# Four groups of instructions in other places between the attention and the expert tiles

## The chip, the cores and the metric
The kernel runs on one core of one Trainium2 chip. The time is the device time of one execution in microseconds (us), the median over several. The core has five engines that run their own instruction streams and meet only at semaphores: TensorE (PE; its weight loads are a second row, PEld), VectorE (DVE), ScalarE (ACT), GpSimd (POOL) and SyncE (SP), which here only starts DMAs.

## The reference
One layer on an input of 8 batches x 256 tokens x 256: normalisation, attention with compressed keys and values (16 heads, a rotary part of 64), then a second normalisation and a mixture of experts, with two residual sums.

```
x = x + attention(layernorm(x))          # 16 heads, 8 batches of 256 tokens
h = layernorm(x)
logits  = h @ gate_w                     # 8 experts
scores  = softmax(logits)
top_w, top_i = top_k(scores, 2)
routed  = sum over the 2 chosen experts of top_w * (silu(h @ w_gate[e]) * (h @ w_up[e])) @ w_down[e]
shared  = (silu(h @ sw_gate) * (h @ sw_up)) @ sw_down      # hidden size 352
x = x + routed + shared
```

## The kernel before, in words
All products are made in three terms of rounded halves: `hi` is a tile rounded by a copy on ACT, `lo` the rest, subtracted on DVE or POOL (`minus_hi`, line 299), and a product is hi*hi + hi*lo + lo*hi (line 226, the helper `three`). So each tile that goes from one product to the next costs an ACT copy (line 1222) and a DVE subtraction.

The first stage is a loop over 64 pairs of heads (g = 0 to 63, eight to a batch). For a pair PE makes scores, ACT the exponentials `probs`, PE turns them (`turn`), ACT and DVE split them (`probs_hi`, `probs_lo`), PE multiplies them with the values (`attend`) into `ps_o`, and `norms` puts the inverse sums into the other half of `ps_o`. ACT copies these to `norm` (`norm_out`), DVE multiplies (`attended`, tile `on`), and `project` follows. `attend` of a pair waits for `norm_done`, since both use one bank. Beside this, the loop carries the router of the batch before: `turn_f` (transposes of the normalised rows `xhat` into `ps_m`), `turned_hi`/`turned_lo` (tile `xf`), `logits`, `gate_max`, `gate_exp` (exponentials `eprob` of 8 columns), `masks` (which two experts), `rank` (products with a triangular matrix that count, for each token, its place in its expert's list), `places` (the row numbers `slots`), and POOL's `scatter` of the rows to DRAM. Weights of the experts are split on the way by `split_hi` on ACT and `split_lo` on DVE (tiles `md_hi`, `md_lo` for the down matrices).

After the loop comes the passage to the tiles, written out by hand on each engine: the shared expert of batches 0 to 3 in chunks (b, m) (`gate_up(b, m)` and `down(b, m)` on PE, `silu` and `unit_hi` on ACT, `units` and `unit_lo` on DVE), and between them the rest of the router: `masks` and `places` of batch 6 (B - 2), all of batch 7 (B - 1), and the table of tiles (`table_counts`, `table_tiles`, `table_rows`, which end with `row_i`, the first row of each tile). SP waits for the table and for the scattered rows and then loads the rows of the 39 tiles (`load_rows`, tile `xg`). Then comes the tile loop (`rows_turn`, `rows_gate_up`, `units_turn`, `rows_down`), the shared expert of batches 4 to 7, and the gathers and stores.

The order on each engine is the order of the written calls, and every engine runs its instructions strictly in that order. An instruction that waits holds all behind it on its engine. ACT's functions Exp and Silu are in different tables: where the function changes, an `ACT_TABLE_LOAD` stands in the order; copies need none.

Of the kernel before, what the change touches and what calls it, by code (L numbers as in the profile page):

```python
# [13 lines left out]
B, S, D = 8, 256, 256  # L14
# [6 lines left out]
PAIRS = B * NP  # L21
# [26 lines left out]
def chunk_rows(m):  # L48
    return min(P, HS - m * P)
# [6 lines left out]
def tile(j):  # L56
    return slice(j * P, (j + 1) * P)
# [57 lines left out]
PARTS = 3 + 4 * KD  # L115
# [344 lines left out]
def splits_upto(L, n):  # L460
    return sum(len(splits) for _, splits in L.parts[0:n + 1])
# [288 lines left out]
def loop(nc, L, d):  # L750
    ev = L.events
    with ExitStack() as ctx:
# [87 lines left out]
        def gu_spot(n):  # L840
            return (L.ps_q, L.ps_s[1], L.ps_t[1])[n % 3]
# [10 lines left out]
        def routed(i, r):  # L852
            return r + 1 if i == B - 1 else r
# [4 lines left out]
        def batch(b):  # L858
            return 0 <= b < B

        def pair(g):
            return 0 <= g < PAIRS
# [77 lines left out]
        def _(pe):  # L940
# [94 lines left out]
            def rank(b):  # L1035
                pe.wait_ge(ev.masks_done, b + 1)

                for n, (terms, at) in enumerate((([(L.before, 0)], 0), ([(L.ones, 0), (L.before, 1)], 1), ([(L.ones, 0), (L.ones, 1)], 2))):
                    for m, (stat, j) in enumerate(terms):
                        last = nc.tensor.matmul(misc[:, 0, at * E:(at + 1) * E], stat[:, :], both[:, j, :], start=m == 0, stop=m == len(terms) - 1)  # L1040
                last.then_inc(ev.rank_full, 1)

            def gate_up(b, m):
                n = ES * b + m
                if m == 0:
                    pe.wait_ge(ev.in_loaded[b], 32)
                if n == 0:
                    pe.wait_ge(ev.qcos_done, PAIRS)
                    pe.wait_ge(ev.part_lo, splits_upto(L, 2))
                elif n == 1:  # L1050
                    pe.wait_ge(ev.exp_done, HEADS)
                elif n >= 3:
                    pe.wait_ge(ev.unit_done, n - 2)
                rows = chunk_rows(m)
                cols = slice(m * P, m * P + rows)
                for g in range(2):
                    last = three(gu_spot(n)[0:rows, g, :],
                                 [(L.sgu_hi[:, g * KD + k, cols], L.sgu_lo[:, g * KD + k, cols],
                                   shared_in[b][:, 0, k, :], shared_in[b][:, 1, k, :]) for k in range(KD)])
                last.then_inc(ev.gu_full, 1)  # L1060

            def down(b, m):
                n = ES * b + m
                pe.wait_ge(ev.ulo_done, n + 1)
                if n == 0:
                    pe.wait_ge(ev.exp_done, HEADS)
                if m == 0 and b >= 2:
                    pe.wait_ge(ev.acc_done, b - 1)
                rows = chunk_rows(m)
                for j in range(NT):  # L1070
                    last = three(ps_d[b % 2][:, j, :], [(u_hi[n % 3][0:rows, tile(j)], u_lo[n % 3][0:rows, tile(j)],
                                                       L.sd_hi[0:rows, m, :], L.sd_lo[0:rows, m, :])],
                                 start=m == 0 and j == 0, stop=m == ES - 1, skip=True)
                last.then_inc(ev.down_done, 1)
# [55 lines left out]
            for g in range(PAIRS):  # L1130
                i, r = divmod(g, NP)
# [48 lines left out]
            logits(B - 1)  # L1180
            down(1, 0)
            gate_up(2, 1)
            down(1, 1)
            gate_up(2, 2)
            rank(B - 1)
            down(1, 2)
            gate_up(3, 0)
            down(2, 0)
# [32 lines left out]
        def _(act):  # L1221
# [12 lines left out]
            def query_hi(g):  # L1234
                act.wait_ge(ev.qrot_done, g + 1)
                if g >= 2:
                    act.wait_ge(ev.s_full, 2 * g - 2)
                copy(q_hi[g % 2][:, :, :], qf[g % 2][:, :, :]).then_inc(ev.qhi_done, 1)

            def exps(h):  # L1240
                act.wait_ge(ev.max_done, h + 1)
                if h >= 3:
                    act.wait_ge(ev.t_full, h - 2)
                for j in range(NT):
                    last = nc.scalar.activation(probs[h % 3][:, j, :], L.ps_s[h % 2][:, j, :], ACT.Exp,  # L1245
                                                bias=nmax[:, h % NH, j:j + 1], accum_out=rsum[:, h % NH, j:j + 1])
                last.then_inc(ev.exp_done, 1)

            def probs_hi(h):
                act.wait_ge(ev.t_full, h + 1)  # L1250
                if h >= 3:
                    act.wait_ge(ev.pv_done, h - 2)
                copy(pT_hi[h % 3][:, :, :], turned[h % 2][:, :, :]).then_inc(ev.phi_done, 1)

            def norm_out(g):
                act.wait_ge(ev.norm_full, g + 1)
                if g >= 1:
                    act.wait_ge(ev.on_done, g)
                copy(norm[:, :], L.ps_o[:, 1, :]).then_inc(ev.norm_done, 1)

            def attended_hi(g):
                act.wait_ge(ev.on_done, g + 1)
                if g >= 2:
                    act.wait_ge(ev.out_done, g - 1)
                copy(o_hi[g % 2][:, :], on[g % 2][:, :]).then_inc(ev.ohi_done, 1)
# [12 lines left out]
            def turned_hi(b):  # L1278
                act.wait_ge(ev.xf_turned, b + 1)
                if b >= 1:  # L1280
                    act.wait_ge(ev.xf_stored, 16 * b)
                    act.wait_ge(ev.logits_full, b)
                copy(xf_hi, misc[:, :, :]).then_inc(ev.xfhi_done, 1)
# [8 lines left out]
            def silu(b, m):  # L1292
                n = ES * b + m
                rows = chunk_rows(m)
                act.wait_ge(ev.gu_full, n + 1)
                if n >= 2:
                    act.wait_ge(ev.unit_done, n - 1)
                nc.scalar.activation(gate[n % 2][0:rows, :], gu_spot(n)[0:rows, 0, :], ACT.Silu).then_inc(ev.silu_done, 1)
# [48 lines left out]
            for g in range(PAIRS):  # L1347
                i, r = divmod(g, NP)
                exps(2 * g + 1)
                if pair(g + 2):  # L1350
                    query_hi(g + 2)
                if pair(g - 1):
                    probs_hi(2 * (g - 1) + 1)
                if pair(g - 2):
                    attended_hi(g - 2)
                if pair(g + 1):
                    exps(2 * (g + 1))
                if pair(g - 1):
                    norm_out(g - 1)
                if r == 4 and batch(i - 1):  # L1360
                    normal_f(i - 1)
                if (r == 0 and i >= 1 or g == 1) and batch(i + 1):
                    prep_normal(i + 1)
                if g in part_round:
                    split_hi(part_round[g])
                if r == 2 and batch(i + 1):
                    prep_x(i + 1)
                if r == 5 and batch(i + 1):
                    prep_k(i + 1)
                if routed(i, r) == 6 and batch(i - 1):  # L1370
                    turned_hi(i - 1)
                if routed(i, r) == 7 and batch(i - 1):
                    gate_exp(i - 1)
                if pair(g + 4):
                    swap(g + 4)
                probs_hi(2 * g)
            probs_hi(HEADS - 1)
            attended_hi(PAIRS - 2)
            silu(0, 0)
            norm_out(PAIRS - 1)  # L1380
            silu(0, 1)
            unit_hi(0, 0)
            attended_hi(PAIRS - 1)
# [40 lines left out]
        def _(dve):  # L1424
# [3 lines left out]
            split_lo = part_lo(nc, L, dve)  # L1428
# [91 lines left out]
            def tokens(b):  # L1520
                if b == 1:
                    dve.wait_ge(ev.cleared, 16)
                if b >= 2:
                    dve.wait_ge(ev.scattered[b % 2], 64 * (b // 2))
                vec.tensor_scalar(xhat_of[b][:, :, D], L.token[:, :], float(b * TOP * S), None, ALU.add).then_inc(ev.tags_done, 1)
# [59 lines left out]
            def unit_lo(b, m):  # L1585
                n = ES * b + m
                rows = chunk_rows(m)
                dve.wait_ge(ev.uhi_done, n + 1)
                if n >= 3:
                    dve.wait_ge(ev.down_done, n - 2)  # L1590
                minus_hi(u_lo[n % 3][0:rows, :], unit[n % 2][0:rows, :], u_hi[n % 3][0:rows, :]).then_inc(ev.ulo_done, 1)
# [66 lines left out]
            for g in range(PAIRS):  # L1658
                i, r = divmod(g, NP)
# [57 lines left out]
            units(1, 1)  # L1717
            places(B - 2)
            tokens(B - 1)
            unit_lo(1, 0)  # L1720
            units(1, 2)
            split_lo(PARTS + 3)
            turned_lo(B - 1)
            accumulate(0)
            unit_lo(1, 1)
# [175 lines left out]
```

## Time and profile before

| what | us |
|---|---|
| median of 3 runs | 628.88 (627.64 to 630.49) |
| the profiled execution | 629.82 |
| its span, first to last instruction | 628.1 |
| PE busy | 605.3 (96%) |
| ACT busy | 475.0 (76%) |
| DVE busy | 467.8 (74%) |
| POOL busy | 410.2 (65%) |
| mean granted clock of PE | 0.984 |

Times in the rows are us from the start of the span. A row of the timeline has the start, the time, the engine, the line of the kernel, the operation, output and inputs by their names (buffer numbers left out), the sizes and the count; in brackets stands the idle time of the engine just before it and what ended it. The granted clock is a share of 2.4 GHz: 1.00 is full speed, 0.50 is 1.2 GHz.

### The profile page before, as it was taken

To read this page: it belongs to the slowest core of one execution; us is meant where nothing else is said; L and a number is where in the kernel's file an instruction comes from. 1 tells how busy PE (TensorE), PEld (TensorE's weight loads), DVE (VectorE), ACT (ScalarE), POOL (GpSimd) and SP (SyncE) were. 2 spreads that over 40 slices of the span, in tenths; PEclk is the share of its full clock that TensorE was granted. 3 is DMA by queue.
4 is the path that set the end of the run, shared out by engine and by line. 5 is a ranking of instruction groups with operands and counts; after the bars stand their busy time and mean duration, and the time that the engine had idled before them with its cause. 6 is when DMAs were issued, how large, how long until landed. Compare 5 with 4: busy or idle time off the path is not lost. (4 is left out here: it accounts for less than half of the span.)

```text
span 628.1 us, 15730 instructions
## 1 busy us (share of the span) xinstructions
PE 605.3 (96%) x4916; PEld 591.3 (94%) x4916; DVE 467.8 (74%) x1406; ACT 475.0 (76%) x1331; POOL 410.2 (65%) x455
## 2 busy tenths in 40 slices
PE   8998999999999999999999999999979989999995
PEld 8888999999999999999999999999978979999994
DVE  6667786877886878788688887778666676666486
ACT  4779999898988989889898898979864335556531
POOL 1467897786897889789789978978613204444400
PEclk9998999999999999999999999999999889999998
DMA  9792000000001001000100100020603155444292
GB/s 259 238 345 41 2 1 3 2 1 35 11 10 43 11 18 43 10 19 3 43 18 10 43 9 19 9 78 11 184 2 118 51 173 166 124 132 120 86 320 83
DMA packets 34024, 45.41 MB, mean 72 GB/s; under 512 B 4056, under 2 KB 29112, under 8 KB 33944
## 3 DMA queue, kind: packets, MB, share of 16 engines
q1 hardware_dynamic: 29160, 34.56, 17.6%
q0 software_dynamic: 3408, 9.34, 4.6%
q8 instruction: 42, 0.69, 0.5%
q10 hardware_dynamic: 1376, 0.50, 0.3%
q14 instruction: 38, 0.31, 0.2%
HBM read 27.57 MB, written 16.82 MB: 71 GB/s over the span
## 5 line engine op out<-in xcount | busy, mean ns | idle before, releaser
L1245 ACT ACTIVATE probs<-ps_s,nmax 128x256 f32<-128x256 f32 x256 | 119.1, 477 | 10.8 <-DVE nmax L1439 10.7
L1785 POOL TENSOR_TENSOR qswap<-qswap,qsin 128x512 f32<-128x512 f32 x64 | 83.3, 1301 | 43.6 <-ACT qswap L1222 43.6
L226 PE MATMUL ps_q<-xa,wq_hi 128*128 128x256 f32 x512 | 101.0, 295 | 3.7 <-DVE qf L1434 3.7
L1439 DVE TENSOR_REDUCE nmax<-ps_s 128x2 f32<-128x512 f32 x128 | 86.8, 678 | 9.3 <-PE ps_s L226 8.6
L1222 ACT ACTIVATE pT_hi<-ps_t 128x512 fp32r<-128x512 f32 x128 | 76.7, 599 | 17.0 <-PE ps_t L978 15.6
L1788 POOL TENSOR_TENSOR qf<-qf,qswap 128x512 f32<-128x512 f32 x64 | 82.7, 1292 | 10.5 <-DVE qf L1434 6.5
L1792 POOL TENSOR_TENSOR q_lo<-qf,q_hi 128x512 fp32r<-128x512 f32 x64 | 82.9, 1296 | 5.8 <-ACT q_hi L1222 5.8
L226 PEld LDWEIGHTS ps_q<-xa,wq_hi 128*128 128x128 f32 x512 | 79.9, 192 | 5.5 <-DVE qf L1434 3.3
L299 DVE TENSOR_TENSOR pT_lo<-ps_t,pT_hi 128x512 fp32r<-128x512 f32 x128 | 81.9, 681 | 1.5 <-ACT pT_hi L1222 1.5
L226 PE MATMUL ps_o<-pT_hi,kv_hi 128*128 128x256 f32 x256 | 76.7, 300 | 2.5 <-ACT norm L1222 2.5
L226 PE MATMUL ps_s<-kT_hi,q_hi 128*128 128x256 f32 x256 | 77.6, 303 | 0.9 <-ACT probs L1245 0.9
L978 PE MATMUL ps_t<-ident,probs 128*128 128x128 f32 x512 | 76.8, 273 | 1.3 <-DVE pT_lo L299 1.3
L1222 ACT ACTIVATE qswap<-ps_q 32x512 f32<-32x512 f32 x128 | 75.6, 590 | 3.3 <-PE ps_q L226 1.0
L1813 POOL DMA_INDIRECT routed_out<-yb,to x39 | 37.4, 959 | 57.7 <-DVE to L1574 55.1
L226 PE MATMUL ps_q<-xa,wq_lo 128*128 128x256 f32 x256 | 73.0, 285 | 0.0
L226 PE MATMUL ps_s<-kT_hi,q_lo 128*128 128x256 f32 x256 | 71.9, 281 | 0.0
L226 PE MATMUL ps_s<-kT_lo,q_hi 128*128 128x256 f32 x256 | 71.8, 280 | 0.0
L226 PE MATMUL ps_o<-pT_hi,kv_lo 128*128 128x256 f32 x256 | 71.5, 279 | 0.0
L226 PE MATMUL ps_o<-pT_lo,kv_hi 128*128 128x256 f32 x256 | 71.4, 279 | 0.0
L978 PEld LDWEIGHTS ps_t<-ident,probs 128*128 128x128 f32 x512 | 59.4, 141 | 1.7 <-issue 1.7
L1796 POOL TENSOR_TENSOR o_lo<-on,o_hi 128x256 fp32r<-128x256 f32 x64 | 47.3, 739 | 17.9 <-ACT o_hi L1222 17.5
L1434 DVE TENSOR_TENSOR qf<-ps_q,qcos 128x512 f32<-128x512 f32 x64 | 43.7, 683 | 15.8 <-ACT qswap L1222 15.6
(337 smaller groups left out, 1914.5 us busy)
## 6 DMA issues: line engine op xcount, KB each, us to landing
xg<-routed_in SPq DMA_DIRECT2D x39, 129.0 KB, 2.2
normal_turned<-xf SPq DMA_DIRECT2D x8, 512.0 KB, 2.8
wq_raw<-Wq_dram SPq DMA_DIRECT2D x16, 192.0 KB, 4.5
x<-x_dram SPq DMA_DIRECT2D x8, 256.0 KB, 5.7
xa<-normal_turned SPq DMA_DIRECT2D x4, 512.0 KB, 5.5
mgu_hi<-routed_out SPq DMA_DIRECT2D x4, 512.0 KB, 5.2
mgu_lo<-routed_out SPq DMA_DIRECT2D x4, 512.0 KB, 7.9
out_dram<-x SPq DMA_DIRECT2D x8, 256.0 KB, 2.9
```

Of the source, the lines that this page charges most:

```text
L226: last = nc.tensor.matmul(out, stat, mov, start=start and n == 0, stop=stop and n == len(terms) - 1, skip_group_check=skip)
L299: return vec.tensor_tensor(lo, src, hi.bitcast(F32), ALU.subtract)
L978: last = nc.tensor.transpose(turned[h % 2][:, c, tile(j)], probs[h % 3][:, j, tile(c)], L.ident[:, :])
L1222: copy = lambda out, src: nc.scalar.activation(out, src, ACT.Copy)
L1245: last = nc.scalar.activation(probs[h % 3][:, j, :], L.ps_s[h % 2][:, j, :], ACT.Exp, bias=nmax[:, h % NH, j:j + 1], accum_out=rsum[:, h % ...
L1434: vec.tensor_tensor(qf[g % 2][:, :, :], L.ps_q[:, :, :], L.qcos[:, :].unsqueeze(1).to_broadcast([P, 2, S]), ALU.mult).then_inc(ev.qcos_don ...
L1439: vec.tensor_reduce(nmax[:, h % NH, :], L.ps_s[h % 2][:, :, :], AX.X, ALU.max, negate=True).then_inc(ev.max_done, 1)
L1785: gp.tensor_tensor(qs, qs, L.qsin[:, :].unsqueeze(1).to_broadcast([P, 2, S]), ALU.mult).then_inc(ev.qrot_part, 1)
L1788: gp.tensor_tensor(to, to, qs, ALU.add).then_inc(ev.qrot_done, 1)
L1792: gp.tensor_tensor(q_lo[g % 2][:, :, :], qf[g % 2][:, :, :], q_hi[g % 2][:, :, :].bitcast(F32), ALU.subtract).then_inc(ev.qlo_done, 1)
L1796: gp.tensor_tensor(o_lo[g % 2][:, :], on[g % 2][:, :], o_hi[g % 2][:, :].bitcast(F32), ALU.subtract).then_inc(ev.olo_done, 1)
L1813: gp.indirect_dma_start(ys[:, :], bass.IndirectOffsetOnAxis(to[:, j:j + 1], 0), yb[j % 3][:, :], None).then_inc(ev.y_stored[j % 3], 16)
```

## The change
Four calls change places; no call is added or taken away, and no wait of a call is changed. On PE `rank(B - 1)` goes ahead of `down(1, 1)` and `gate_up(2, 2)`. On ACT `gate_exp(B - 2)` leaves the loop (it ran at pair g = 62) and stands behind it, and `norm_out(PAIRS - 1)` goes ahead of `silu(0, 0)`. On DVE `split_lo(PARTS + 3)` goes ahead of `unit_lo(1, 0)` and `units(1, 2)`.

```diff
--- before.py
+++ after.py
@@ -1180,9 +1180,9 @@
             logits(B - 1)
             down(1, 0)
             gate_up(2, 1)
+            rank(B - 1)
             down(1, 1)
             gate_up(2, 2)
-            rank(B - 1)
             down(1, 2)
             gate_up(3, 0)
             down(2, 0)
@@ -1369,15 +1369,16 @@
                     prep_k(i + 1)
                 if routed(i, r) == 6 and batch(i - 1):
                     turned_hi(i - 1)
-                if routed(i, r) == 7 and batch(i - 1):
+                if routed(i, r) == 7 and batch(i - 1) and i < B - 1:
                     gate_exp(i - 1)
                 if pair(g + 4):
                     swap(g + 4)
                 probs_hi(2 * g)
             probs_hi(HEADS - 1)
             attended_hi(PAIRS - 2)
+            gate_exp(B - 2)
+            norm_out(PAIRS - 1)
             silu(0, 0)
-            norm_out(PAIRS - 1)
             silu(0, 1)
             unit_hi(0, 0)
             attended_hi(PAIRS - 1)
@@ -1717,9 +1718,9 @@
             units(1, 1)
             places(B - 2)
             tokens(B - 1)
+            split_lo(PARTS + 3)
             unit_lo(1, 0)
             units(1, 2)
-            split_lo(PARTS + 3)
             turned_lo(B - 1)
             accumulate(0)
             unit_lo(1, 1)
```

ACT, end of the attention loop and start of the passage. `eprob` are the router's exponentials of batch 6, `norm` the copy of the last pair's inverse sums, `gate` the first of the shared expert. The order on ACT before:

```order
L469 ACTIVATE md_hi<-md_raw 88x2x256 x2
L1288 ACTIVATE eprob,esum<-ps_m,lmax 128x8 x2
L1222 ACTIVATE pT_hi<-ps_t 128x512
...
L1222 ACTIVATE o_hi<-on 128x256
L1298 ACT_TABLE_LOAD
L1298 ACTIVATE gate<-ps_q 128x256
L1222 ACTIVATE norm<-ps_o 128x256
L1298 ACTIVATE gate<-ps_s 128x256
```

The same place on ACT after:

```order
L469 ACTIVATE md_hi<-md_raw 88x2x256 x2
L1222 ACTIVATE pT_hi<-ps_t 128x512
L1245 ACTIVATE probs,rsum<-ps_s,nmax 128x256 x2
...
L1222 ACTIVATE o_hi<-on 128x256
L1288 ACTIVATE eprob,esum<-ps_m,lmax 128x8 x2
L1222 ACTIVATE norm<-ps_o 128x256
L1298 ACT_TABLE_LOAD
L1298 ACTIVATE gate<-ps_q 128x256
```

The exponentials went from behind the weight split to behind `o_hi`, and `norm` from between the first two gates to ahead of the table load.

DVE, the passage, at batch 6's places and the split `xf` of batch 7. The order on DVE before:

```order
L1518 COPY xhat_f<-row_f 128x2
L1525 TENSOR_SCALAR xhat_g<-token 128x2
L299 TENSOR_TENSOR u_lo0<-unit1,u_hi0 128x256
L1583 TENSOR_TENSOR unit1<-ps_t1,gate1 96x256
L477 TENSOR_TENSOR md_lo<-md_raw,md_hi 88x2x256 x2
L299 TENSOR_TENSOR xf<-ps_m,xf 128x512
L1596 TENSOR_TENSOR x2<-ps_s0,x2 128x512
```

The same place on DVE after:

```order
L1519 COPY xhat_f<-row_f 128x2
L1526 TENSOR_SCALAR xhat_g<-token 128x2
L477 TENSOR_TENSOR md_lo<-md_raw,md_hi 88x2x256 x2
L299 TENSOR_TENSOR u_lo0<-unit1,u_hi0 128x256
L1584 TENSOR_TENSOR unit1<-ps_t1,gate1 96x256
L299 TENSOR_TENSOR xf<-ps_m,xf 128x512
L1597 TENSOR_TENSOR x2<-ps_s0,x2 128x512
```

The subtraction `md_lo` went from right ahead of `xf` to ahead of `u_lo` and the unit of chunk (1, 2).

PE, the passage, between the up products of chunk (2, 1) (`ps_s`) and of (2, 2) (`ps_t` from `wo_hi`; the shared expert's inputs of batch 2 lie in `wo_hi`). The order on PE before:

```order
L226 MATMUL ps_s<-wo_hi,sgu_lo 128x256
L226 MATMUL ps_t<-sd_hi,u_hi 128x256
...
L226 MATMUL ps_t<-sd_hi,u_lo 128x256
L226 MATMUL ps_t<-wo_hi,sgu_hi 96x256 x2
L226 MATMUL ps_t<-wo_hi,sgu_lo 96x256
...
L226 MATMUL ps_t<-wo_hi,sgu_lo 96x256
L1040 MATMUL ps_m<-both,before 128x8
L1040 MATMUL ps_m<-both,ones 128x8
L1040 MATMUL ps_m<-both,before 128x8
L1040 MATMUL ps_m<-both,ones 128x8 x2
```

The same place on PE after:

```order
L226 MATMUL ps_s<-wo_hi,sgu_lo 128x256
L1040 MATMUL ps_m<-both,before 128x8
L1040 MATMUL ps_m<-both,ones 128x8
L1040 MATMUL ps_m<-both,before 128x8
L1040 MATMUL ps_m<-both,ones 128x8 x2
L226 MATMUL ps_t<-sd_hi,u_hi 128x256
...
L226 MATMUL ps_t<-sd_hi,u_lo 128x256
L226 MATMUL ps_t<-wo_hi,sgu_hi 96x256 x2
L226 MATMUL ps_t<-wo_hi,sgu_lo 96x256
...
L226 MATMUL ps_t<-wo_hi,sgu_lo 96x256
L226 MATMUL ps_t<-sd_hi,u_hi 128x256
```

The counting products (line 1040) went ahead of `down(1, 1)` (`ps_t` from `u_hi`, `u_lo`) and of `gate_up(2, 2)`.

## Rows read from the trace of the kernel before

**Rows 1.** Stretch 510:594: us, busy us (x instructions) of each engine, clock, DMA share, GB/s
```profile
510.00:594.00 84.00, 83.81 (x622) 81.17 (x621) 52.99 (x190) 48.19 (x154) 35.95 (x38) 1.00 0.46 139
```

**Rows 2.** PE's waits, 455 to 530: total us, times, longest us
```profile
PE ps_o L226 <- ACT norm L1222: 2.1, 1, 2.1
...
PE ps_t L226 <- DVE u_lo L299: 2.0, 1, 2.0
```

**Rows 3.** PE by time: start us, us, engine, line, operation, tiles, count, [idle before <-releaser]
```profile
481.45 0.66 PE L1025 MATMUL ps_m<-ident,xhat_g 128*128 128x128 f32 x4
...
484.57 0.27 PE L226 MATMUL ps_m<-gw_hi,xf 128*128 128x8 f32 x1 [1.04 <-DVE xf L299]
...
493.34 0.17 PE L1040 MATMUL ps_m<-both,before 128*128 128x8 f32 x1
...
506.23 0.69 PE L1081 MATMUL ps_m<-ident,xg 128*128 128x128 f32 x2 [1.75 <-DMA xg<-routed_in]
```

**Rows 4.** DVE by time, 481 to 503
```profile
481.73 0.42 DVE L299 TENSOR_TENSOR u_lo<-unit,u_hi 128x256 fp32r<-128x256 f32 x1 [1.20 <-ACT u_hi L1222]
...
482.60 1.31 DVE L477 TENSOR_TENSOR md_lo<-md_raw,md_hi 88x512 fp32r<-88x512 f32 x2
...
483.84 0.68 DVE L299 TENSOR_TENSOR xf<-ps_m,xf 128x512 fp32r<-128x512 f32 x1
...
486.48 0.17 DVE L1484 TENSOR_REDUCE lmax<-ps_m 128x2 f32<-128x16 f32 x1 [1.03 <-PE ps_m L226]
...
489.28 0.17 DVE L1504 TENSOR_TENSOR choice<-both,choice 128x16 f32<-128x16 f32 x1
...
494.00 0.17 DVE L1510 TENSOR_TENSOR where<-ps_m,base 128x16 f32<-128x16 f32 x1 [3.88 <-PE ps_m L1040]
...
502.95 0.17 DVE L1558 CAST row_i<-row_of 1x39 int32<-1x39 f32 x1
```

**Rows 5.** SyncE's wait for the scattered rows (line 926)
```profile
L926 SPq EVENT_SEMAPHORE  x1: 28/28/28, 502.7 to 502.7; - x1
```

**Rows 6.** Three stretches, as rows 1; the clock follows POOL's busy time
```profile
485.00:495.00 10.00, 10.00 (x61) 10.00 (x61) 4.08 (x32) 3.64 (x10) 1.16 (x1) 0.66 0.22 81
...
495.00:500.00 5.00, 5.00 (x44) 5.00 (x44) 4.78 (x16) 1.49 (x4) 3.28 (x4) 1.00 0.16 57
...
505.00:510.00 5.00, 3.77 (x19) 3.74 (x20) 3.12 (x15) 1.07 (x3) 0.00 (x0) 0.66 0.43 109
```

**Rows 7.** ACT by time, 459 to 482
```profile
459.52 0.27 ACT L1288 ACTIVATE eprob<-ps_m,lmax 128x8 f32<-128x8 f32 x1 [1.44 <-DVE lmax L1484]
...
460.03 0.59 ACT L1222 ACTIVATE pT_hi<-ps_t 128x512 fp32r<-128x512 f32 x1
...
460.51 0.48 ACT L1245 ACTIVATE probs<-ps_s,nmax 128x256 f32<-128x256 f32 x1
...
467.38 0.41 ACT L1222 ACTIVATE o_hi<-on 128x256 fp32r<-128x256 f32 x1
...
467.80 1.28 ACT L1298 ACT_TABLE_LOAD   x1
...
469.10 0.38 ACT L1298 ACTIVATE gate<-ps_q 128x256 f32<-128x256 f32 x1
...
469.38 0.38 ACT L1222 ACTIVATE norm<-ps_o 128x256 f32<-128x256 f32 x1
...
482.14 0.60 ACT L1222 ACTIVATE xf<-ps_m 128x512 fp32r<-128x512 f32 x1 [0.17 <-PE ps_m L1025]
```

**Rows 8.** DVE by time, 459 to 479
```profile
459.41 0.68 DVE L1439 TENSOR_REDUCE nmax<-ps_s 128x2 f32<-128x512 f32 x1
...
471.58 0.42 DVE L1466 TENSOR_TENSOR on<-ps_o,norm 128x256 f32<-128x256 f32 x1 [0.74 <-PE ps_o L226]
...
474.13 0.42 DVE L1583 TENSOR_TENSOR unit<-ps_t,gate 96x256 f32<-96x256 f32 x1 [0.57 <-ACT gate L1298]
...
479.03 0.16 DVE L317 TENSOR_SCALAR var_f<-mean_f 128x2 f32<-128x2 f32 x1
```

## The prediction

> **What bounds the kernel now.** I read first the busy time by stretch. In the stage of the 39 expert tiles TensorE (PE) is busy for 83.81 of 84 us [rows 1], so that stage can't absorb or return anything: it starts when its first tile is there and ends a fixed time later. The passage before it is another matter. The waits of PE between 455 and 530 us [rows 2] start with 2.1 us for the copy `norm` and 2.0 us for VectorE's (DVE's) `u_lo`; a third is 1.75 us for the DMA of the first tile, `xg` [rows 3]. In the last two PE waits for a chain that runs on DVE; so for the start of the tiles the question is not how much PE idles, but what that chain waits for. I followed it backwards. The transposes of the first tile start at 506.23 behind that DMA wait [rows 3], 3.1 us after DVE finished `row_i`, the row numbers that its load reads (502.95 + 0.17) [rows 4]; the scattered rows were there by then, since SyncE's wait for them ended at 502.7 [rows 5]. `row_i` stands at the end of table work that starts with `where` at 494.00, and from there DVE has nothing to wait for. `where`, the first step of the places of the last batch (7), had DVE idle for 3.88 us, released by PE's counting products [rows 4], which start at 493.34 [rows 3]. But the masks that these count were ready with `choice` at 489.45 (489.28 + 0.17) [rows 4]. About 4 us of the chain are thus only PE's order of work. A second view is PE's granted clock [rows 6]: 1.00 (2.4 GHz) at 495:500 with 44 products, but 0.66 over 485:495 with 61, where 88 would fit, and 0.66 at 505:510. 0.66 over 10 us is 6.8 us at 1.2 GHz, and the 27 missing products are worth 3.1 us. So PE runs most of the stretch ahead of the counting at half clock; the clock fell there after a 1.04 us wait and in the middle of the narrow, eight-column router products [rows 3].
>
> **The change part by part.** Nothing is added or removed; four groups change places.
>
> 1. Router exponentials of batch 6 on ScalarE (ACT). They stood at 459.52 with 1.44 us idle before them, and the next `probs` pair came at 460.51 [rows 7]. That pair also needs the row maxima, which DVE ends at 459.41 + 0.68 = 460.09 [rows 8]; DVE's own order doesn't change there. So `probs` starts at 460.13: 0.38 gained, not 1.44, and what follows (DVE's sums, PE's transposes) moves by that amount.
>
> 2. The copy `norm` before the table load. `o_hi` started at 467.38 [rows 7] and now starts at 467.00. Behind it come the four small exponential instructions, which take 0.51 us as a group (459.52 to the `pT_hi` at 460.03) [rows 7]; then `norm`. One ACT start follows the last by 0.28 (469.10 to 469.38) to 0.42 (467.38 to 467.80) [rows 7]; with 0.33 this gives 467.00 + 0.33 + 0.51 = 467.84 against 469.38 [rows 7]: PE's attention products go on 1.54 us earlier, and 0.6 of the 2.1 us of [rows 2] stays. The exponentials find the exponential table still in place, since the load that they stood ahead of is now behind them. Price: the table load and the first `gate` behind it come at 469.56 instead of 469.10 [rows 7]. It meets DVE's `unit` and `u_lo` work ahead of the last `on`; that chain moves later by 0.46, then catches up, since `unit_hi` follows the second gate, which lost its place only by 0.2. I work out that `on`, at 471.58 [rows 8], comes at 471.23, 0.35 earlier. From there DVE had one more wait, 0.57 us before the `unit` of 474.13 [rows 8], for a gate of PE products that now come 1.54 us earlier. Both together: the masks of batch 6, the residual and `var_f` (479.03 [rows 8]) move by 0.9 to 1.0, not 1.54. `var_f` feeds GpSimd's power, ACT's normalisation and PE's transposes at 481.45, which followed the products ahead of them with hardly a pause (no wait is noted in their row [rows 3]). So here the gain is cut to 1.0: transposes at 480.45, with PE waiting 0.5 more than before.
>
> The row of the load says 1.28 us, and the first gate starts 1.30 after it [rows 7]. The Trainium skill (ScalarE: Activation LUTs, "What ACT_TABLE_LOAD costs") gives about 2.66 us for a switch of sets, drain included. By that the gate after the load would be 1.4 us later and DVE's chain the same; the trace does not agree, and the sum goes by the row.
>
> 3. The weight split (`md_lo`) on DVE. It took 1.31 us from 482.60 and stood right ahead of `xf_lo`, which began at 483.84 [rows 4]; the logits waited for that till 484.57 with PE idle 1.04 us [rows 3]. Now the split runs before `unit_lo`, where DVE had 1.2 us idle waiting for ACT ([rows 4], before 481.73; the split falls at 479.5 to 480.8 in the new times, and the rounded half that it needs comes from ACT before its normalisation, as now). Then `xf_lo` follows ACT's `xf`, which starts 0.69 after the transposes (482.14 [rows 7] against 481.45): 481.14, and 0.60 and 0.68 later `xf_lo` is done, 482.46 with the hand-overs. PE's gate and up products between transposes and logits end at about 482.5. So the wait of 1.04 goes entirely and the logits start at 482.5, 2.07 earlier than 484.57.
>
> 4. The counting products (rank) before `down(1,1)` and `gate_up(2,2)` on PE. From the logits to `lmax` the trace has 1.91 us (484.57 to 486.48, partly at half clock); at 44 products in 5 us, 0.114 each [rows 6], the twelve products and the reader's start take 1.5, so `lmax` comes at 484.1, and the masks, 2.97 us after it as before (486.48 to 489.45 [rows 4]), at 487.05. PE fills this with `down(1,0)` and `gate_up(2,1)`, 18 products, 2.1 us, to 486.1 and then waits 0.9 us: a new wait, behind which all PE work is queued. The counting starts at 487.1, `where` at 487.78 (0.66 later, as 493.34 to 494.00). That is 6.2 us earlier than 494.00. Behind it the DVE chain needs `down(1,2)` for the second accumulation at 490.6: PE gives it at 490.5 (24 products after 487.6), just in time. The slots, the scatter, `row_i` (496.9) and the load all move by the same 6.2, and the first tile's transposes come at 500.0. PE reaches them at about 498.3 and still waits 1.7, so DVE's chain and not PE sets this start. Without the move of rank alone, the counting would start at 488.2: of the 6.2 us, 1.1 belong to this edit at full clock, and much more (over 3) at half clock.
>
> Bounds of what the trace doesn't show. If PE has 2.4 GHz everywhere in the passage: 6.2; and if the second fall, at 505:510, stays away too, up to 1.5 more (0.66 over 5 us is 3.4 us at half clock [rows 6], at the 0.45 per us of case D). If the clock falls as before: 4.0 to 4.9 (next part). I take 6.2, because the wait that preceded the fall is taken away.
>
> Sum: the profiled execution took 629.82 us with a span of 628.1; minus 6.2 is 623.6. The median of the unprofiled runs, 628.88, is 0.9 lower; from it the sum is 622.7. I take the middle, 623.2.
>
> **The rivals.**
>
> A. The clock still falls. For it: the eight-column products, 12 of the logits and 5 of the count, now stand closer together, with new waits of 0.5 to 0.8 us ahead of the transposes and 0.9 us ahead of the count. Against: the 1.04 us wait directly ahead of the logits is gone, and the 2.1 us wait for `norm` [rows 2] was followed by no fall. In this case the 24 products to `down(1,2)` take about 0.2 instead of 0.114 each (28 products fit in the 3.2 us at full clock of 485:495, which leaves 33 for the 6.8 slow ones [rows 6]) and the accumulation comes about 2 us late; the gain is 4.0 to 4.9, in the middle 4.4: 625.4 from the profiled time, 624.5 from the median. The Trainium skill (TensorE: Matmul & The Clock Gate, Part 1) says that the activity monitor is free-running and does not start over with the kernel. By that rule some executions of the same program would fall and others not, which would also spread the runs; the three of before lie 2.9 us apart, and no trace here shows the cause.
>
> B. The logits do not come earlier, because the chain to `xf_lo` has a step that I mis-sized; only the move of rank pays. PE would count at 490.1 instead of 493.3, and the accumulation behind it is late by 0.7: 2.6 gained, 627.2 or 626.3. Against it: every wait in the chain has its row.
>
> C. No change: another stage takes the gain back, for instance the gathers at the end, or the copy is late for another reason, or the edits don't do what they say. Against: PE in the tiles is busy throughout [rows 1]. The time is then 628.9, give or take 1.5.
>
> D. Slower. The place is the start of the tiles: PE still waits twice there, 0.6 and 1.7 us, and the first tiles hold transposes and waits. If the clock falls there and does not come back at 509, as it did, but stays low over several tiles, each us at half clock costs about 0.45 us of work (3.1 for 6.8 [rows 6]). From 14 us of it on the whole gain is lost; at 25 us the cost is 11.3, and the time 5.1 above the median before, 634.0. Against: in [rows 6] the second fall was over within 5 us, and the tiles are dense.
>
> **How the numbers follow.** Forecast 50% (its own range 621.5 to 624.8), A 27%, B 10%, C 8%, D 5%. A measurement of this kernel tells a change from about 0.5%, 3.1 us: faster means under 625.7. That holds for the forecast and nearly all of A, and for little else: 0.79. Within 0.5% are B, C and an edge of A: 0.16. Slower: 0.05. The range goes from 621.0 (the second fall partly gone) to 626.4, where B ends from the median.
>
> **What would show it.** In the profile after: `norm` at about 467.8, ahead of the table load, and PE's wait for it under 1 us; `var_f` near 478.1 and the transposes at 480.4; logits at 482.5 with no wait before them; a new PE wait of about 0.9 us before the counting products, starting at 487.1; DVE's 3.88 us before `where` gone; the first tile's transposes at 500.0. The granted clock in 483 to 492 decides between forecast and A. The forecast is wrong if the first tile starts later than 503, or if it starts at 500 and the span doesn't follow.

## The result and the profile after

The changed kernel takes 624.40 us (median of 6, 622.67 to 625.89) against 629.43 us of before (6 runs, 627.64 to 630.49): ratio 0.9925, 95% interval 0.9905 to 0.9944. Forecast were 623.2 and a chance of 0.79 for faster. Two later sets of runs on two different chips gave ratios of 0.9909 (0.9873 to 0.9945) and 0.9912 (0.9879 to 0.9946). The profiled execution took 624.46 us with a span of 622.7.

The waits of PE between 450 and 525 us, to be read against [rows 2] and the brackets of [rows 3]:

```profile
PE ps_m L1081 <- DMA xg<-routed_in: 1.8, 1, 1.8
PE ps_o L226 <- ACT norm L1222: 0.9, 1, 0.9
PE ps_t L978 <- DVE pT_lo L299: 0.9, 1, 0.9
PE ps_m L1040 <- DVE choice L1505: 0.8, 1, 0.8
PE ps_m L1025 <- ACT xhat_g L1275: 0.6, 1, 0.6
PE ps_t L226 <- DVE u_lo L299: 0.4, 1, 0.4
```

PE's wait for `norm` is 0.9 instead of 2.1 us, the one for `u_lo` 0.4 instead of 2.0, and the wait ahead of the logits is not in the list. Two waits are new or longer: 0.8 for the counting products (line 1040) and 0.6 for the transposes (line 1025). The one ahead of the first tile is still there, 1.8 us.

PE by time, the rows that answer to [rows 3]:

```profile
479.50 0.66 PE L1025 MATMUL ps_m<-ident,xhat_g 128*128 128x128 f32 x4 [0.60 <-ACT xhat_g L1275]
...
481.57 0.27 PE L226 MATMUL ps_m<-gw_hi,xf 128*128 128x8 f32 x1
...
486.14 0.27 PE L1040 MATMUL ps_m<-both,before 128*128 128x8 f32 x1 [0.84 <-DVE choice L1505]
...
499.38 0.44 PE L1081 MATMUL ps_m<-ident,xg 128*128 128x128 f32 x2 [1.82 <-DMA xg<-routed_in]
```

DVE by time, for [rows 4] and [rows 8] (line numbers are one higher):

```profile
458.57 0.68 DVE L1440 TENSOR_REDUCE nmax<-ps_s 128x2 f32<-128x512 f32 x1
...
470.30 0.42 DVE L1467 TENSOR_TENSOR on<-ps_o,norm 128x256 f32<-128x256 f32 x1
...
472.19 0.41 DVE L1584 TENSOR_TENSOR unit<-ps_t,gate 96x256 f32<-96x256 f32 x1
...
477.08 0.16 DVE L317 TENSOR_SCALAR var_f<-mean_f 128x2 f32<-128x2 f32 x1
...
478.49 1.28 DVE L477 TENSOR_TENSOR md_lo<-md_raw,md_hi 88x512 fp32r<-88x512 f32 x2
...
480.82 0.69 DVE L299 TENSOR_TENSOR xf<-ps_m,xf 128x512 fp32r<-128x512 f32 x1
...
483.11 0.17 DVE L1485 TENSOR_REDUCE lmax<-ps_m 128x2 f32<-128x16 f32 x1 [0.66 <-PE ps_m L226]
...
485.91 0.17 DVE L1505 TENSOR_TENSOR choice<-both,choice 128x16 f32<-128x16 f32 x1
...
486.90 0.17 DVE L1511 TENSOR_TENSOR where<-ps_m,base 128x16 f32<-128x16 f32 x1 [0.15 <-PE ps_m L1040]
...
496.03 0.17 DVE L1559 CAST row_i<-row_of 1x39 int32<-1x39 f32 x1
```

ACT at the table load, for [rows 7]:

```profile
466.14 0.41 ACT L1222 ACTIVATE o_hi<-on 128x256 fp32r<-128x256 f32 x1
466.45 0.26 ACT L1288 ACTIVATE eprob<-ps_m,lmax 128x8 f32<-128x8 f32 x1
...
466.93 0.39 ACT L1222 ACTIVATE norm<-ps_o 128x256 f32<-128x256 f32 x1
467.34 1.28 ACT L1298 ACT_TABLE_LOAD   x1
468.63 0.38 ACT L1298 ACTIVATE gate<-ps_q 128x256 f32<-128x256 f32 x1
```

All of this run is 0.84 us ahead before the change begins: the last row maxima in the loop come at 458.57 instead of 459.41 [rows 8], after instructions that are the same in both kernels. In the twelve further profiles below that point lies between 457.1 and 461.0 us; two profiles of the changed kernel differ there by 3.35 us. So I count the passage from there. From these maxima to the first tile's transposes it took 506.23 - 459.41 = 46.82 us before and 499.38 - 458.57 = 40.81 after: 6.0 us less. PE's busy time splits this into two halves. The first line is before, the second after; both have 289 products:

```profile
459.41:506.23 46.82, 38.39 (x289) 36.93 (x289) 32.08 (x130) 21.67 (x55) 11.17 (x13) 0.92 0.17 60
```
```profile
458.57:499.38 40.81, 35.32 (x289) 33.88 (x288) 31.95 (x130) 21.11 (x54) 11.55 (x13) 1.00 0.20 69
```

PE idles 5.5 instead of 8.4 us, 2.9 less, and is busy 3.1 us less with the same products, at a clock of 1.00 instead of 0.92.

The rest of the way did not stay the same. Stretches of the profile after, as [rows 6] (the clock is the third number from the end):

```profile
466.00:476.00 10.00, 9.07 (x77) 8.86 (x76) 6.44 (x30) 5.80 (x18) 1.46 (x2) 1.00 0.15 47
485.00:495.00 10.00, 9.16 (x78) 8.95 (x77) 9.21 (x43) 3.77 (x11) 4.12 (x4) 1.00 0.19 69
500.00:507.50 7.50, 7.46 (x32) 6.77 (x31) 4.02 (x13) 2.23 (x7) 0.00 (x0) 0.54 0.65 189
510.00:590.00 80.00, 79.96 (x600) 77.87 (x599) 48.98 (x177) 45.81 (x147) 37.08 (x39) 1.00 0.42 126
```

The clock stays at 1.00 where it was 0.66 before (485:495), but from 500 to 507.5 it is 0.54, that is 6.9 us at 1.2 GHz, where before had 3.4. From the first tile to the end this execution needs 123.3 us and the one before 121.9. The balance of the two profiles: 0.8 by the start, 6.0 in the passage, 1.5 given back from the tiles on: 5.4 us of span. The longer fall is not all of the 1.5, as the further profiles of both kernels show below.

### The profile page after: what moved, and what is told of

Same layout as the page of the kernel before. It is cut to its first block and busy times, and to the rows that moved or that the text cites. A ratio compares the mean times of both kernels' runs of the same rounds, so it can differ in the third digit from the quotient of the medians.

```text
span 622.7 us, 15730 instructions
## 1 busy us (share of the span) xinstructions
PE 601.9 (97%) x4916; PEld 587.2 (94%) x4916; DVE 469.0 (75%) x1406; ACT 474.8 (76%) x1331; POOL 410.4 (66%) x455
## 3 DMA queue, kind: packets, MB, share of 16 engines
HBM read 27.57 MB, written 16.82 MB: 71 GB/s over the span
## 5 line engine op out<-in xcount | busy, mean ns | idle before, releaser
L1435 DVE TENSOR_TENSOR qf<-ps_q,qcos 128x512 f32<-128x512 f32 x64 | 43.7, 683 | 15.6 <-ACT qswap L1222 15.4
```

What stands on the lines that cost most here:

```text
L1435: vec.tensor_tensor(qf[g % 2][:, :, :], L.ps_q[:, :, :], L.qcos[:, :].unsqueeze(1).to_broadcast([P, 2, S]), ALU.mult).then_inc(ev.qcos_don ...
```

## The experiments

Each ratio is to runs of the kernel before on the same chip. For every execution the mean granted clock is known, and with it its time at 1.2 GHz: (1 - clock) x span x 2; the clock is given to 0.001, so this comes in steps of about 1.25 us. "Passage" is the time from the last row maxima to the first tile, from the profile.

| kernel | ratio (95%) | median us | us at 1.2 GHz, median | passage us |
|---|---|---|---|---|
| before, 67 runs in three sets | 1 | 629.5 | 17.6 | 46.82, 46.76, 46.79 |
| changed, 18 runs in three sets | 0.9925, 0.9909, 0.9912 | 624.2 | 8.7 | 40.81, 40.80, 40.75 |
| ACT edits alone | 0.9954 (0.9928 to 0.9979) | 625.7 | 13.7 | 42.75 |
| split alone | 0.9956 (0.9925 to 0.9988) | 625.3 | 15.0 | 44.10 |
| count alone | 0.9983 (0.9954 to 1.0012) | 626.9 | 15.6 | 43.35 |
| ACT and split | 0.9927 (0.9899 to 0.9955) | 623.6 | 12.4 | 41.62 |
| count one place later | 0.9927 (0.9901 to 0.9952) | 624.5 | 14.9 | 40.65 |
| changed, filled at the tiles | 0.9907 (0.9874 to 0.9940) | 622.9 | 7.4 | 40.76 |
| before, filled at the logits | 0.9976 (0.9953 to 1.0000) | 627.5 | 16.2 | 45.14 |
| count later, filled twice | 0.9895 (0.9863 to 0.9928) | 621.8 | 6.8 | 40.53 |

**The ACT edits alone.** The edit:

```diff
-                if routed(i, r) == 7 and batch(i - 1):
+                if routed(i, r) == 7 and batch(i - 1) and i < B - 1:
                     gate_exp(i - 1)
...
+            gate_exp(B - 2)
+            norm_out(PAIRS - 1)
             silu(0, 0)
-            norm_out(PAIRS - 1)
```

> Only the two edits on ACT: the router's exponentials of batch 6 behind the loop, the copy norm ahead of the table load. Theory (the chain sets the start of the tiles; each edit pays by what it moves there): PE's wait for norm falls from 2.1 to about 0.9 us, the transposes of batch 7 come 1.0 earlier, the logits 1.0 earlier and still after a 1 us wait behind the weight split, the clock falls as before, and DVE's 3.9 us before `where` stay. Time 1.0 us under before, ratio 0.998. Rival (PE's waits count): 1.5 us or more, ratio 0.9975 or less.

The steps came as forecast: the transposes come 20.94 us after the row maxima, before 22.04, so 1.1 earlier, and the logits still wait. But the clock did not fall. PE ahead of the logits and the clock after them in this profile:

```profile
482.93 0.27 PE L226 MATMUL ps_m<-gw_hi,xf 128*128 128x8 f32 x1 [1.05 <-DVE xf L299]
```
```profile
466.00:476.00 10.00, 9.07 (x78) 8.86 (x77) 6.17 (x29) 5.83 (x17) 1.47 (x2) 1.00 0.12 32
483.00:495.00 12.00, 12.00 (x103) 12.00 (x104) 8.98 (x46) 5.14 (x14) 4.35 (x6) 1.00 0.24 89
```

The wait of 1.05 us is there, the eight-column products are there, and the clock stays at 1.00. So the two together do not make it fall in every execution, and my reason for the forecast ("the wait that preceded the fall is taken away") is not the whole of it. The passage is 4.1 us shorter, 1.1 by order and 3 by the clock of this execution. The time is 3.7 us under before, where 1.0 was expected, and the interval just leaves out the expected 0.998. The number is in the rival's range, but the order of work moved the chain by the theory's 1.1 us; the rest goes with the clock (13.7 us at 1.2 GHz in the median against 17.6).

**The split alone.**

```diff
+            split_lo(PARTS + 3)
             unit_lo(1, 0)
             units(1, 2)
-            split_lo(PARTS + 3)
```

> Only the weight split ahead of unit_lo(1, 0) on DVE. Theory: the wait ahead of the logits goes, they start 1.0 us earlier. If the clock's fall hung on that wait, PE stays at 2.4 GHz up to the counting products, which then come 4 us earlier: ratio 0.9935. Rival (the clock falls in any case, by the narrow products): 1.0 us, ratio 0.998.

From the transposes to the logits it took 2.07 us instead of 3.12: 1.05 us by order, as forecast. At the logits the clock stayed up. But this execution had a fall that the first profile of before did not have, behind the 2.13 us wait for `norm` (466:476):

```profile
466.00:476.00 10.00, 8.39 (x58) 8.42 (x59) 4.84 (x26) 3.88 (x10) 1.03 (x2) 0.83 0.01 2
480.00:495.00 15.00, 14.85 (x126) 14.45 (x125) 11.77 (x51) 8.69 (x22) 7.57 (x8) 1.00 0.25 89
```

This fall made DVE's chain up to the transposes 1.5 us late. The ratio lies between the two expectations, and its interval holds both, so the time decides nothing between them.

**The counting products alone.**

```diff
+            rank(B - 1)
             down(1, 1)
             gate_up(2, 2)
-            rank(B - 1)
```

> Only the counting products ahead of down(1, 1) and gate_up(2, 2) on PE. Theory: the clock falls as before; the products come at about 490.1 against 493.3, without a wait; the second accumulation is 0.7 late; 2.6 us gained, ratio 0.996. Rival (PE's order does not matter): no gain, ratio 1.000.

The passage shrank by 3.5 us in the profile, but part of that is a shorter fall (clock 0.79 over 484:492, that is 3.4 us at 1.2 GHz instead of 6.8). The time, 0.9983 where 0.996 was expected, does not tell it from no change. The logits started at 484.87, and `where` followed 5.76 us later:

```profile
490.63 0.17 DVE L1510 TENSOR_TENSOR where<-ps_m,base 128x16 f32<-128x16 f32 x1 [0.58 <-PE ps_m L1040]
```

At full clock that way takes 5.33 us with the count in its new place (the changed kernel) and 6.34 in its old one (the next run). So here a fall of 3.4 us cost the chain 0.4 us. A fall of the same length behind the logits of the kernel before cost it 1.5 (7.87 us, 486.48 to 494.35, in the first of the two further profiles below). The earlier count is thus worth about 2 us where the clock falls behind the logits, and 1.1 at `where` (0.8 at the first tile) where it does not. The prediction had 1.1 at full clock and "over 3" at half clock, for a fall twice as long.

**The changed kernel without the move of the count.** The edit is the last diff taken back.

> The changed kernel with the counting products put back behind gate_up(2, 2). Theory: the clock stays up in the passage as in the changed kernel, the new PE wait of 0.84 us goes, the counting starts 1.1 us later than in the changed kernel, and so does the first tile: ratio to before 0.9943 (the changed kernel 0.9925). Rival (the rank edit is the larger part of the gain): 3 us later than the changed kernel, 0.997.

The counting starts 28.69 us after the maxima instead of 27.57, 1.1 later as forecast, and the first tile 0.8 later (41.62 against 40.81): of the 1.1, 0.1 went between the count and `where`, and 0.2 in DVE's wait for the second accumulation, both in the changed kernel. In the time nothing of it is seen: 0.9927 against 0.9909 to 0.9925. The clock is 1.00 in this passage up to 497.0, shortly ahead of PE's wait for the first tile, and falls there:

```profile
496.50:504.00 7.50, 5.96 (x27) 5.64 (x28) 5.13 (x18) 1.49 (x4) 0.00 (x0) 0.54 0.35 92
```

**The changed kernel once more**, on the chip of the next three.

> The changed kernel once more, on the chip of the next three. Every execution has its own count of us at 1.2 GHz, (1 - mean clock) x span x 2, and before loses 0.46 us for each. Theory: the changed kernel gains 3 us by its order of work at equal clock, and 1 to 2 us more since the clock falls less often in the passage: ratio 0.9925, 3 us under before at equal us of low clock. Rival (all of it is the clock): no difference at equal us of low clock.

Ratio 0.9909; the passage 40.80. Its clock is 1.00 from 482 to 512, at the start of the tiles too, and from the first tile to the end it needs 122.3 us, 1.0 less than the first profile. Over all 18 runs of the changed kernel the median is 8.7 us at 1.2 GHz, over the 67 of before 17.6. The 0.41 us per us that a line through the 67 runs gives makes about 3.6 us of this difference. The comparison at equal clock is thin, since the two hardly overlap: between 10 and 14.5 us at 1.2 GHz lie 14 runs of before with a median of 625.8 and 4 of the changed kernel with 624.4. 11 of the 18 have 10 us or less, and 1 of the 67.

So the expected 3 us at equal clock were not found in the times: it is 1.4 here, and the 18 runs lie on average 1.6 us under the line of the kernel before (for most of them the line has to be drawn on below its own points). Against that the kernel "ACT and split" lies 3.0 under the line, and "count one place later" 2.9. The rival, that all is clock, is out by the passage, but how the time divides into order and clock is not settled.

The stretch from the first tile to the end has a part in this. It took 121.9, 122.3 and 122.3 us in the three profiles of before, with 3.4, 6.8 and 6.8 us at 1.2 GHz around the first tile, and 123.3, 122.3 and 122.4 in the three of the changed kernel, with 6.9, none and none. With the same fall the changed kernel needs 1 us more there, and without a fall as much as before with one. The 20 us from the first tile, before and in this run:

```profile
506.23:526.23 20.00, 19.85 (x133) 18.96 (x134) 12.97 (x47) 10.06 (x32) 4.79 (x5) 0.92 0.70 213
```
```profile
501.77:521.77 20.00, 19.20 (x131) 17.34 (x132) 12.70 (x45) 9.82 (x32) 4.79 (x5) 1.00 0.67 206
```

At full clock PE idles 0.8 us there (1.3 in the third profile) instead of 0.15. So part of what the passage gained is given back behind it. Which order of work costs it there was not tested.

**The count one place later.**

```diff
-            rank(B - 1)
             down(1, 1)
+            rank(B - 1)
             gate_up(2, 2)
```

> The changed kernel with the counting products between down(1, 1) and gate_up(2, 2). They are ready when their masks are, which is after down(1, 1) would end, so they start at the same time as in the changed kernel. Theory: PE's new wait of 0.84 us ahead of them shrinks to 0.1, the first tile comes at the same time after DVE's last row maxima (40.8 us), or 0.2 earlier, since down(1, 2) comes 0.7 earlier for the second accumulation. Time as the changed kernel or up to 0.5 us less. Rival: the wait counts, 0.8 us less.

The products start at the same 27.57 us, now without PE's wait of 0.84, and the first tile comes 0.15 earlier. The wait has moved: PE's wait for `u_lo` is 1.0 us instead of 0.4. The time is 624.5 against 623.7 on the same chip, where the same or up to 0.5 less was expected; the intervals overlap. Its median of time at 1.2 GHz is 14.9 us against 8.1 of the changed kernel beside it. The new wait of the change costs the start of the tiles 0.15 us at most, since DVE's chain is what ends last.

**Idle products at the start of the tiles.**

```diff
+            def filler(count):
+                pe.wait_ge(ev.x2_done, B)
+                for n in range(count):
+                    nc.tensor.matmul(L.ps_y[:, 0, :], L.sgu_hi[:, 0, 0:P], L.sgu_lo[:, 0, 0:S], start=True, stop=True)
...
             down(3, 0)
+            filler(15)
             rows_turn(0)
```

> The changed kernel with 15 idle products (128x128 weights, 256 columns, into a bank that nobody reads) in the 1.8 us in which PE waits for the first tile. They add work only. Theory (a fall of the clock at the tile start follows the waits just before it, and costs 0.45 us for each us at 1.2 GHz): the clock stays at 1.00 through 500:510, the us of low clock fall by about 7 and the time by 1.5 to 3 us against the changed kernel. Rival (the fall has nothing to do with the wait): the same clock, and time as the changed kernel or up to 0.5 more.

PE in this profile, with the idle products in the place of the wait:

```profile
496.26 1.95 PE L1088 MATMUL ps_y<-sgu_lo,sgu_hi 128*128 128x256 f32 x15
498.18 0.44 PE L1081 MATMUL ps_m<-ident,xg 128*128 128x128 f32 x2
```

The clock stayed at 1.00, but so it did in the unfilled kernel's second and third profiles, and the medians differ by 0.8 us, where 1.5 to 3 were expected, with intervals that overlap. The time at 1.2 GHz hardly moved either (7.4 against 8.1 us, expected about 7 less). This neither shows nor refutes the theory that the wait brings the fall; its price is not borne out.

**Idle products ahead of the logits, in the kernel before.** `filler(8)` ahead of `logits(B - 1)`.

> The kernel before with 8 idle products in PE's 1.04 us wait ahead of the logits of batch 7. Theory (the fall at 485 follows this wait): the clock stays up through 483:495 in most executions, the high cluster of times (630 to 632) thins out, median 1.5 to 3 us under before. Rival (the fall comes in any case, by the narrow products or by chance of position): distribution as before, ratio 1.000.

In the profile there is no fall after the logits (483:495), but one behind the wait for `norm` (466:476):

```profile
466.00:476.00 10.00, 7.87 (x54) 7.66 (x53) 3.86 (x12) 4.58 (x10) 1.46 (x2) 0.83 0.01 2
483.00:495.00 12.00, 11.91 (x102) 11.71 (x101) 8.94 (x45) 6.84 (x16) 4.35 (x6) 1.00 0.24 89
```

Of the 12 runs none is above 630 us, where 8 of the 21 unfilled ones on this chip are (25 of all 67). The median is 2.0 us lower and the ratio's interval just touches 1. That speaks for the theory, which had 1.5 to 3 us, without settling it: the one profile has no fall behind the logits, but neither has that of the ACT edits alone, where the wait was left as it was.

**Two more profiles of the kernel before.**

> The kernel before, unchanged, one more profile. Theory (the place where the clock falls is not fixed by the program): the passage from DVE's last row maxima in the loop to the first tile takes 43.7 us where the clock stays at 1.00 and 46.8 where it falls as in the first profile; the fall may be absent from 485:492 or stand at another place. Rival (the program fixes it): 0.5 at 486 to 492 again, and 46.8.

> The kernel before once more, one more profile, with the same expectations as the look before it.

The first of them, around the two waits:

```profile
469.00:476.00 7.00, 5.71 (x35) 5.74 (x36) 2.38 (x5) 2.87 (x8) 0.73 (x1) 0.76 0.01 2
486.00:492.00 6.00, 5.52 (x34) 5.52 (x35) 4.10 (x25) 3.26 (x10) 1.89 (x2) 0.72 0.43 156
```

and the second:

```profile
469.00:476.00 7.00, 6.72 (x44) 6.75 (x45) 3.18 (x11) 1.88 (x6) 0.73 (x1) 0.76 0.01 2
486.00:492.00 6.00, 6.00 (x40) 6.00 (x40) 3.09 (x24) 3.26 (x9) 1.16 (x1) 0.72 0.37 134
```

There are two falls now, 3.4 us at 1.2 GHz each (0.24 x 7 x 2 and 0.28 x 6 x 2): one behind the wait for `norm`, where the first profile had none, and one behind the logits as in the first, half as long. In the first of the two profiles the logits started here:

```profile
486.48 0.27 PE L226 MATMUL ps_m<-gw_hi,xf 128*128 128x8 f32 x1 [1.05 <-DVE xf L299]
```

The second fall follows 1.5 us later (in the very first profile 1.0 after the logits' start). So the program does not fix whether the clock falls at a wait nor for how long, but the places are the same few. The passage is 46.76 and 46.79, as long as the first: three profiles of before, 6.8 us at 1.2 GHz in each, and three of the changed kernel with none. The theory's 43.7 us at full clock was not seen in any profile of before.

All fourteen profiles together show something that the forecast did not have. In the six without the ACT edits (where PE waits 2.1 us for `norm`) the clock fell between that wait and the count every time. In the eight with them (where it waits 0.9) it never did, also not in the one where the wait of 1.05 us ahead of the logits was left. So the smaller share of low clock in the passage goes with the ACT edits in these profiles. No run shows how they bring it about.

**Both ideas together**: the count one place later, 7 idle products ahead of `down(3, 0)` and 15 ahead of the first tile, and beside it the changed kernel again.

> The changed kernel with the counting products between down(1, 1) and gate_up(2, 2), 7 idle products ahead of down(3, 0) and 15 ahead of the first tile's transposes. Theory: first tile at 40.65 us after DVE's last row maxima, clock 1.00 to 510, fewer us of low clock than the changed kernel (8 to 11): median 622.5 to 623.2, 0.5 to 1.5 under the changed kernel on the same chip. Rival (the idle products only delay): as the changed kernel or more.

> The changed kernel, beside the last one on its chip. Theory: first tile again 40.8 us after DVE's last row maxima, ratio 0.991 to 0.9925. Rival: a ratio above 0.994, if the two chips so far were kind to it.

The first tile came at 40.53 and 40.75 us, and the medians are 621.8 and 623.2 on one chip, 1.4 apart as expected (0.5 to 1.5). It is the lowest median of all, but its interval (0.9863 to 0.9928) overlaps with the other's. The changed kernel's 0.9912 is as its theory had it.

## Why the prediction was right

By its own steps, each as us from the last row maxima (459.41 in the forecast's times):

| step | forecast | measured |
|---|---|---|
| `norm` starts | 8.43 | 8.36 |
| `var_f` (478.05) | 18.6 | 18.51 |
| transposes of batch 7 | 21.04 | 20.93 |
| logits | 23.1 | 23.00 |
| masks ready | 27.6 | 27.51 |
| counting products | 27.7 | 27.57 |
| `where` | 28.37 | 28.33 |
| `row_i` ends | 37.5 | 37.63 |
| first tile | 40.6 | 40.81 |

- The exponentials' new place gave `probs` 0.39 (0.38 forecast), `norm` comes 1.6 earlier with it, and of this 1.1 was left at the transposes, since DVE's chain of batch 6 holds them, as forecast. The new PE wait there is 0.60 (0.5 more was said). PE's wait for `norm` is 0.93, not the forecast's 0.6: the sum took the copy's whole gain off the wait, though PE comes to it 0.4 earlier too.
- The split's move took the whole wait ahead of the logits; its price, a later `u_lo`, was nil: `u_lo` follows at 479.78, just when ACT has given it its half.
- The count: 0.84 us of new wait (0.9 forecast), and the chain from `where` to `row_i` as long as before but for 0.2. Its own share at full clock is 0.8 at the first tile, not 1.1: the term was the start of the counting, and 0.3 of it were lost behind, 0.1 up to `where` and 0.2 at the second accumulation, which the forecast had just in time.
- The shares by order of work add up: 1.1 (ACT), 1.05 (split), 0.8 (count), together 2.9 to 3.0 of the 6.0, which is what PE idles less. The other 3.1 are the clock, as the forecast took it (2.4 GHz everywhere in the passage), and as PE's busy time shows. Rival A, that it still falls there, is out by the three profiles of the changed kernel, not by the time: 624.4 is nearer to its 624.5 than to the forecast's 623.2. Rivals B and D are out by the passage and the time, and so is C as a whole; a part of C, that a later stage takes some of the gain back, did happen.

What was off is the time by 1.2 us (623.2 against 624.40), and two reasons. The first is that the stage of the tiles "can't absorb or return anything": from the first tile to the end the profiles take 121.9 to 122.3 us before and 122.3 to 123.3 after. The bounds named the fall at the tiles, and I took it as unchanged, 3.4 us; in the first profile after it is 6.9, in the two others it is not there at all, and these still need 0.5 to 0.6 us more than the first profile of before. So of the 1.5 us given back, about 1 goes with this fall and the rest does not.

The second is the clock. "The 2.1 us wait for `norm` was followed by no fall" was true of one execution and false as an argument: of the five later profiles with that wait in them, four (the two further ones of before, the split alone, the filled kernel before) have a fall behind it, and one (the count alone) has none. In the changed kernel this wait is 0.9 us and no profile has a fall there. And the wait taken away ahead of the logits, the forecast's reason, was still there in the ACT edits alone, with no fall. That the clock term of 3.1 us came as forecast owes something to luck, since the reason given for it does not hold. What makes the clock fall in one execution and not in the next stays open. The Trainium skill says (TensorE: Matmul & The Clock Gate, Part 1) that the monitor is free-running. That falls come and go between executions of one program agrees with it; beside it stand the three profiles of the kernel before, with 0, 3.4 and 3.4 us at 1.2 GHz behind the wait for `norm` and 6.8, 3.4 and 3.4 behind the logits.

## What to carry to other kernels

Follow the chain that ends last before a dense stage back to its first step, and ask at each wait whether what it waits for was ready and only queued late: 3 us of the passage here lay in an order of calls, and every time in the table above held within 0.25 us. A wait of an engine off this chain (PE's new one ahead of the count) can be moved without effect: it came back behind `u_lo`. Follow the gain to the end as well: of the 6.0 us of the passage 4.5 were left at the end of the first profile. Where the clock falls in some executions and not in others, one profile does not show how often: take several, measure lengths from an anchor inside the program, and look at the clock of every run. Busy time and idle time of the same products tell order from clock.

## What the hardware showed that I had not expected

- The unchanged kernel has runs from 625.1 to 634.0 us. A straight line through 67 runs gives 0.41 us for each us at 1.2 GHz (0.46 in the largest set of 35, correlation 0.85, and 0.36 and 0.35 in the two others); the forecast had 0.45.
- The length of the passage at equal clock repeats to 0.1 us (40.75 to 40.81 in the changed kernel), while the way to it varies by almost 4 us over all fourteen profiles (457.1 to 461.0), with the same instructions up to there.
- A fall of the same 3.4 us behind the logits cost the chain to `where` 1.5 us with the count in its old place and 0.4 in its new one, where fewer products stand between.
- Idle products in PE's waits did no measurable harm to the time in any of the three kernels that had them, nor is a gain shown.
